# Edge stream of a graph-attention layer: node rows picked by TensorE from two float32r parts of the table, in 4 blocks by 32 sides

## The chip, the core and the metric

The kernel runs on one core of one Trainium2 chip. A core has a matrix engine (TensorE: PE for its matmuls, PEld for its weight loads), three engines for elementwise work (VectorE or DVE, ScalarE or ACT, GpSimd or POOL) and a sequencer that mostly starts transfers (SyncE or SP). They run their own instruction streams and meet at semaphores. The metric is the device time of one execution in microseconds (us). Lower is better.

## What is computed

A small language-model tower with two layers: a hashed n-gram embedding, a phase attention, a graph attention with experts, a second attention and a feed-forward part. The change lies in the graph attention. It has 16,384 nodes (16 x 1024) and 262,144 random edges, and one loop edge for each node is added:

```
h = (x_flat @ W_gat).reshape(M, HEADS, NUM_EXPERTS)        # M = 16384 nodes, 4 heads x 4
a_src = (h * att_src).sum(-1);  a_dst = (h * att_dst).sum(-1)
e = leaky_relu(a_src[src] + a_dst[dst], negative_slope=0.2)
e_max = segment_max(e, dst);  ee = exp(e - e_max[dst]);  denom = segment_sum(ee, dst)
msg = h[src] * (ee / (denom[dst] + 1e-16))[:, :, None]
agg = segment_sum(msg, dst).reshape(M, 16) + b_gat
scores = layernorm(agg).reshape(M, HEADS, NUM_EXPERTS).mean(1)   # the 2 best of 4 experts, softmax of them
out = sum over experts of g * (gelu(x @ W1[e] + b1[e]) @ W2[e] + b2[e])
```

For each of the 278,528 edges the 16 numbers of row `h[src]` are needed.

## The kernel before

**Ahead of the edge stream**, `front` makes the embedding, the first attention and the node table (24 numbers for a node: 16 of h, 4 of a_src, 4 of a_dst), and sorts the edges by their destination on VectorE. The sorted edges lie on 128 partitions, 2176 columns each. The same function holds `split(j)` (line 460), which writes 32 of the 128 table columns (tiles of 128 nodes) into `parts` for TensorE: three bf16 numbers that add up to one float32 number, made by five VectorE instructions, four times in all.

**The edge stream** (`edge_stream`, line 768) goes over the 2176 columns in 68 chunks of 32 (`CH`). A running maximum, sum and message are carried along each partition by scans. A chunk's 32 columns of rows come in two ways:

- 24 columns (`GC`) are fetched by POOL, one indirect DMA each of 128 rows of the table in DRAM (line 857). The buffer `got` holds two chunks. POOL may fill it for chunk c+2 once VectorE has let go of chunk c (`s_free`).
- 8 columns (`PC`) are picked by TensorE. A node number is written as within + 1024 x side: a place inside a block set of 8 x 128 nodes (`BLOCKS` = 8), and one of 16 sides (`SIDES`). For a column of 128 edges ScalarE makes a one-hot matrix of 1024 x 128 in bf16 (`pick`): the square of the difference between the wanted and each own number (line 871, 8 instructions for 4 columns), then relu(1 - square) (line 875, one instruction for 4 columns). TensorE multiplies it with each of the 3 parts (line 937): 8 blocks x 3 parts = 24 products of 256 columns for a column of edges, 192 for a chunk. This gives the rows of all 16 sides. VectorE multiplies them by the edge's own side (`es_own`, line 1015; `take`, line 1019), which picks one of 16, and adds over the sides (line 1021). Two columns are a `pair`, four pairs a chunk, each with a PSUM bank of its own. A pair's products wait until the take of the same pair of the chunk before has read the bank (`s_taken`).

The picked rows of chunk c+1 are made while chunk c is worked on. SyncE broadcasts the wanted numbers of a whole chunk (8 x 128 numbers to all partitions, 512 KB) into one of two halves of `away` (line 817) when ScalarE has finished with it.

**The order is written by hand**, a `turn` for each engine. On TensorE: pair 0 of the next chunk, experts 0 and 1 (`expert`, line 944, float32), pair 1, the counts of 16 columns (`count`, line 956, one-hot matrices in bf16, which VectorE makes at lines 1039 and 1040), bias and output products of the experts (lines 979 and 950), experts 2 and 3, pair 2, outputs, pair 3, the counts of 16 columns. On VectorE: scores and maximum of chunk c, one-hots for two counts, takes 0 and 1 of chunk c+1, exponentials from ScalarE, message, `s_free` (line 1077), 16 scans (line 1079), one-hots for two counts, takes 2 and 3 of chunk c+1 and their attention sums. 64 of the 68 turns carry expert work and run as a loop of two turns.

Behind the edge stream come a join of the partitions' runs and the second layer.

Of the kernel before, what the change touches and what calls it, by code (L numbers as in the profile page):

```python
# [14 lines left out]
ALU = mybir.AluOpType  # L15
ACT = mybir.ActivationFunctionType
AX = mybir.AxisListType
F32 = mybir.dt.float32
BF16 = mybir.dt.bfloat16
I32 = mybir.dt.int32  # L20
U32 = mybir.dt.uint32

P = 128
# [6 lines left out]
ST = 4  # L30
# [121 lines left out]
BLOCKS = 8  # L152
SIDES = TILES // BLOCKS
ROWS_T = CHUNKS * PC
# [19 lines left out]
def front(nc, mem, ids, tables, edges, consts, weights, sorted_keys, table_dram):  # L174
# [11 lines left out]
    hash_space, late, parts, xts = mem["hash_space"], mem["late"], mem["parts"], mem["xts"]  # L186
    with ExitStack() as ctx:
# [8 lines left out]
        low = hash_space[0:B]  # L196
# [3 lines left out]
        rows = sb("rows", [P, TILES, 3], I32)  # L200
        ring = sb("ring", [P, RINGS, 3, ST, D])
# [14 lines left out]
        rest = sb("rest", [P, BLOCKS, 4, 16])  # L216
# [179 lines left out]
        def _(dve):  # L396
# [63 lines left out]
            def split(j):  # L460

                tiles = slice(j * 32, j * 32 + 32)
                block_rows = tab[:, tiles, 0:16].rearrange("p (h k) f -> p k h f", k=BLOCKS)
                part = lambda n: parts[:, n, :, j * 64:j * 64 + 64].rearrange("p k (h f) -> p k h f", f=16)
# [130 lines left out]
            def prepare(part):  # L595

                if part == 0:
# [5 lines left out]
                    ch.step(v.tensor_scalar(few, pe_cols(key), 10, SIDES - 1, ALU.logical_shift_right, ALU.bitwise_and)); ch.settle()  # L603
# [163 lines left out]
def edge_stream(nc, mem, sorted_keys, table_dram, state_dram, y_dram):  # L767
# [6 lines left out]
    with ExitStack() as ctx:  # L774
# [8 lines left out]
        turned = pick[:, 0, 1].rearrange("p k n -> p (k n)").bitcast(F32)[:, 0:5 * P]  # L783
        own = sb("es_own", [P, PC, SIDES], F32)
        prod = sb("es_prod", [P, 2, SIDES, 16], F32)
        att = sb("es_att", [P, 2, PC, 16], F32)
# [7 lines left out]
        msg = sb("es_msg", [P, CH, 16], F32)  # L794
# [4 lines left out]
        p_got = ps("es_pgot", [P, PAIRS, 512])  # L799
# [7 lines left out]
        rows = sorted_keys[0:ROWS_T * P].rearrange("(n c) -> n c", c=PC * P)  # L807

        @block.sync
        def _(sp):  # L810
# [5 lines left out]
            def load(n, r):  # L816
# [1065 lines left out]
```

## Time and profile before

| | us |
|---|---|
| median of 3 runs | 5086.44 |
| lowest and highest | 5078.35, 5090.78 |
| the profiled execution's span | 5093.1 |
| PE busy (matmuls) | 3045.9 (60%) |
| PEld busy (weight loads) | 2318.6 (46%) |
| DVE busy | 2806.7 (55%) |
| ACT busy | 2362.3 (46%) |
| POOL busy | 2224.4 (44%) |

The profiled execution has no time of its own beside its span, which is 6.7 us above the median of the runs. A busy share says how full an engine is over the whole span. No engine is above 60%, so the shares alone don't say what sets the time. In the rows further down, "idle before, releaser" is the time in which an engine stood still ahead of an instruction, and what ended it. "issue" means that nothing in the profile released it.

### The profile page before, as it was taken

What the parts mean: (1) busy time and instruction counts of PE and PEld (TensorE: products, weight loads), DVE (VectorE), ACT (ScalarE), POOL (GpSimd) and SP (SyncE); (2) the same over time, 40 slices, a digit from 0 to 9 for tenths busy, and PEclk for the clock granted to TensorE, in tenths of its full rate; (3) what the DMA queues carried; (4) which work ended last, traced back from release to release, by engine and by line L of the source; (5) the groups of instructions that cost most, each with busy time, mean ns of one, the idle gap of its engine ahead of it and who ended that gap; (6) DMA issues with size and microseconds to landing.
All of it is one profiled execution on the core that took longest, in us unless ns stands there. A gap on an engine that the chain in (4) does not pass through costs nothing. (4 is left out here: it accounts for less than half of the span.)

```text
span 5093.1 us, 63233 instructions
## 1 busy us (share of the span) xinstructions
PE 3045.9 (60%) x21149; PEld 2318.6 (46%) x21149; DVE 2806.7 (55%) x5784; ACT 2362.3 (46%) x4288; POOL 2224.4 (44%) x2218
## 2 busy tenths in 40 slices
PE   3656663666566566566566566566566566544775
PEld 2445542554454454455455455455455455432443
DVE  8857883445445445445445445445445445467986
ACT  3636655444444444444444444444434434404886
POOL 7865613334434434434434434434434434426530
PEclk7657775777777777777777777777777777766887
DMA  1111101111111111111111111111111111112101
GB/s 58 24 22 20 22 7 44 24 23 27 31 23 27 31 23 27 31 23 27 31 23 27 31 23 27 31 23 27 31 23 27 31 23 27 25 27 75 38 19 33
DMA packets 157528, 145.13 MB, mean 28 GB/s; under 512 B 71240, under 2 KB 133080, under 8 KB 156776
## 3 DMA queue, kind: packets, MB, share of 16 engines
q1 hardware_dynamic: 88656, 109.49, 6.4%
q0 software_dynamic: 68768, 34.45, 6.2%
q8 instruction: 41, 0.67, 0.1%
q14 instruction: 63, 0.52, 0.0%
HBM read 92.97 MB, written 50.82 MB: 28 GB/s over the span
## 5 line engine op out<-in xcount | busy, mean ns | idle before, releaser
L937 PE MATMUL es_pgot<-hash_space,es_pick 128*128 128x256 bf16 x13056 | 1835.9, 288 | 1423.7 <-issue 1418.8
L857 POOL DMA_INDIRECT es_got<-node_table,late x1632 | 1548.1, 949 | 2127.0 <-DVEq L1077 1649.7
L937 PEld LDWEIGHTS es_pgot<-hash_space,es_pick 128*128 128x128 bf16 x13056 | 1302.8, 101 | 1899.6 <-issue 1742.7
L1019 DVE TENSOR_TENSOR es_prod<-es_pgot,es_own 128x512 f32<-128x512 f32 x272 | 187.7, 690 | 1801.6 <-PE es_pgot L937 1627.7
L871 ACT ACTIVATE es_pick<-es_away,consts 128x512 bf16<-128x512 f32 x1088 | 680.0, 711 | 7.0 <-DMA es_away<-sorted_keys 6.6
L293 POOL DMA_INDIRECT fr_ring<-in_emb,fr_rows x384 | 456.0, 1188 | 209.8 <-issue 112.8
L875 ACT ACTIVATE es_pick<-es_pick,consts 128x4096 bf16<-128x4096 bf16 x136 | 503.6, 3703 | 0.9
L894 ACT ACTIVATE ex_hid<-ex_phid,weights 128x256 f32<-128x256 f32 x128 | 53.6, 470 | 692.7 <-PE ex_phid L944 692.3
L1039 DVE TENSOR_TENSOR es_hot<-es_iota,late 128x1024 bf16<-128x1024 f32 x272 | 331.7, 1219 | 33.4 <-DVE es_st L1079 25.7
L1040 DVE TENSOR_TENSOR es_hot<-es_iota,late 128x1024 bf16<-128x1024 f32 x272 | 330.2, 1214 | 0.0
L894 ACT ACT_TABLE_LOAD x32 | 41.1, 1283 | 559.2 <-PE ex_phid L944 559.2
L910 ACT ACTIVATE ex_y<-ex_py 128x512 f32<-128x512 f32 x64 | 38.2, 597 | 565.0 <-remote 541.2
L1021 DVE TENSOR_REDUCE es_got<-es_prod 128x32 f32<-128x512 f32 x272 | 276.0, 1015 | 39.6
L956 PE MATMUL es_counts<-es_hot 128*128 128x128 bf16 x2176 | 202.2, 264 | 30.7 <-DVE es_hot L1040 23.8
L511 DVE TENSOR_TENSOR fr_space<-fr_space 128x1024 f32<-128x1024 f32 x173 | 211.5, 1223 | 5.4
L1079 DVE TENSOR_TENSOR_SCAN es_st<-es_ex,es_st,es_msg 128x32 f32<-128x32 f32 x1088 | 208.7, 281 | 10.0
L512 DVE TENSOR_TENSOR fr_space<-fr_space 128x1024 f32<-128x1024 f32 x173 | 210.7, 1218 | 0.0
L956 PEld LDWEIGHTS es_counts<-es_hot 128*128 128x128 bf16 x2176 | 186.0, 123 | 43.3 <-issue 33.7
L903 ACT ACT_TABLE_LOAD x64 | 82.1, 1283 | 162.0 <-PE ex_phid L944 162.0
L1347 POOL DMA_INDIRECT bk_ring<-edge_states,node_end x128 | 137.1, 1071 | 38.6 <-issue 32.4
L944 PE MATMUL ex_phid<-xc,weights 128*128 x1024 | 139.5, 279 | 0.0
L950 PE MATMUL ex_py<-weights,ex_hid 128*128 128x64 f32 x1024 | 134.9, 275 | 0.0
(351 smaller groups left out, 4294.6 us busy)
## 6 DMA issues: line engine op xcount, KB each, us to landing
es_away<-sorted_keys SPq DMA_DIRECT2D x68, 512.0 KB
es_got<-node_table,late POOLq DMA_INDIRECT x1632
edge_states<-es_st SPq DMA_DIRECT2D x68, 384.0 KB
expert_outputs<-ex_y SPq DMA_DIRECT2D x64, 256.0 KB
bk_y<-expert_outputs SPq DMA_DIRECT2D x8, 2048.0 KB
fr_ring<-in_emb,fr_rows POOLq DMA_INDIRECT x384
out_dram<-h SPq DMA_DIRECT2D x4, 1024.0 KB, 5.1
late<-in_edges SPq DMA_DIRECT2D x1, 2048.0 KB, 9.3
```

The source lines that it names most:

```text
L293: pool.indirect_dma_start(out=ring[:, r, n, t, :], out_offset=None, in_=tables[n], in_offset=bass.IndirectOffsetOnAxis(ap=rows[:, s * ST + ...
L511: ch.step(v.tensor_tensor(o[:, :, 0, :], left, right, ALU.min))
L512: ch.step(v.tensor_tensor(o[:, :, 1, :], left, right, ALU.max))
L857: pool.indirect_dma_start(out=got[:, r, k, :], out_offset=None, in_=table_dram, in_offset=bass.IndirectOffsetOnAxis(ap=src[:, n, k:k + 1]. ...
L871: a.activation(pick[:, r, half, k], away[:, r, half * 4 * P:half * 4 * P + 4 * P], ACT.Square, bias=C("away")[:, k:k + 1]).then_inc(s_act, 1)
L875: a.activation(pick[:, r, half], pick[:, r, half], ACT.Relu, scale=-1.0, bias=C("ones")).then_inc(s_pick, 1)
L937: mm = pe.matmul(p_got[:, q, c * 256:c * 256 + 256], pick[:, r, q // 2, k, at * P:at * P + P], parts[:, part, k], start=(k == 0 and part = ...
L956: mm = pe.matmul(counts, hot[:, n % 2, 0, k, :], hot[:, n % 2, 1, k, :], start=False, stop=False, skip_group_check=True)
L1021: ch.step(v.tensor_reduce(got[:, r, GC + 2 * q:GC + 2 * q + 2, 0:16], prod[:].rearrange("p c h f -> p c f h"), AX.X, ALU.add)); ch.settle()
L1039: v.tensor_tensor(hot[:, n % 2, 0], repeat(iota, OH), spread(hi[:, at], P), ALU.is_equal)
L1040: v.tensor_tensor(hot[:, n % 2, 1], repeat(iota, OH), spread(lo[:, at], P), ALU.is_equal).then_inc(s_hot, 1)
L1079: ch.step(v.tensor_tensor_scan(st[:, r, 1:, 8 + j], ex[:, 0, :, j // 4], msg[:, :, j], st[:, r, 0, 8 + j:9 + j], ALU.mult, ALU.add))
```

## The change

- The table has two parts instead of three. The first is the float32 number written as float32r (a float32 with a shortened mantissa), the second the rest, again as float32r. `split` is two VectorE instructions.
- A node number is within + 512 x side: 4 blocks of 128 and 32 sides. A product has 512 columns (32 sides x 16), which is a whole PSUM bank. A column of edges takes 4 x 2 = 8 products, a chunk 64. Both operands are float32r, the one-hot matrix too.
- The four banks of `p_got` now hold two pairs, two columns each. So pair q waits for the take of pair q-2, one chunk or half a chunk before, instead of the same pair of the chunk before.
- ScalarE makes 4 squares for 4 columns instead of 8, and the relu goes over 2048 elements for a partition instead of 4096, float32r instead of bf16.
- VectorE's take reads 2 x 512 columns instead of 2 x 256, and adds over 32 sides. The own-side mask is twice as wide.
- `away` holds one chunk in two halves, and SyncE loads halves: 256 KB each, two for a chunk.
- Places in memory: `hash_space` goes, and the hashes lie in `ring`; `msg` lies in `prod`; `turned` lies in `hot`.

The core of the diff:

```diff
-BLOCKS = 8
+BLOCKS = 4
 SIDES = TILES // BLOCKS
+SIDE_BITS = 9
+PARTS = 2
+BANKS = 4
...
-                ch.step(v.tensor_copy(part(0), block_rows)); ch.settle()
-                ch.step(v.tensor_tensor(rest[:], block_rows, part(0), ALU.subtract)); ch.settle()
-                ch.step(v.tensor_copy(part(1), rest[:])); ch.settle()
-                ch.step(v.tensor_tensor(rest[:], rest[:], part(1), ALU.subtract)); ch.settle()
-                ch.step(v.tensor_copy(part(2), rest[:])); ch.settle()
+                ch.step(v.tensor_copy(part(0), block_rows)); ch.settle()
+                ch.step(v.tensor_tensor(part(1), block_rows, part(0).bitcast(F32), ALU.subtract)); ch.settle()
...
-        away = sb("es_away", [P, 2, PC * P], F32)
+        away = sb("es_away", [P, 2, 4 * P], F32)
-        pick = sb("es_pick", [P, 2, 2, BLOCKS, 4 * P], BF16)
+        pick = sb("es_pick", [P, 2, 2, BLOCKS, 4 * P], F32R)
-        p_got = ps("es_pgot", [P, PAIRS, 512])
+        p_got = ps("es_pgot", [P, BANKS, SIDES * 16])
...
-            def load(n, r):
-                sp.dma_start(away[:, r], rows[bass.ds(n, 1), :].broadcast_to([P, PC * P])).then_inc(s_away[r], 16)
+            def load(n, half):
+                sp.dma_start(away[:, half], rows[bass.ds(n * 2 + half, 1), :].broadcast_to([P, 4 * P])).then_inc(s_away[half], 16)
...
-                    a.activation(pick[:, r, half, k], away[:, r, half * 4 * P:half * 4 * P + 4 * P], ACT.Square, bias=C("away")[:, k:k + 1]).then_inc(s_act, 1)
+                    a.activation(pick[:, r, half, k], away[:, half], ACT.Square, bias=C("away")[:, k:k + 1]).then_inc(s_act, 1)
...
-                if not first:
-                    pause(pe, s_taken, (n - 1) * PAIRS + q + 1, s_spent)
+                if not (first and q < 2):
+                    pause(pe, s_taken, n * PAIRS + q - 1, s_spent)
                 for c in range(2):
                     at = (q % 2) * 2 + c
                     for k in range(BLOCKS):
-                        for part in range(3):
-                            mm = pe.matmul(p_got[:, q, c * 256:c * 256 + 256], pick[:, r, q // 2, k, at * P:at * P + P], parts[:, part, k],
-                                           start=(k == 0 and part == 0), stop=(k == BLOCKS - 1 and part == 2))
+                        for part in range(PARTS):
+                            mm = pe.matmul(p_got[:, at], pick[:, r, q // 2, k, at * P:at * P + P], parts[:, part, k],
+                                           start=(k == 0 and part == 0), stop=(k == BLOCKS - 1 and part == PARTS - 1))
...
-                ch.step(v.tensor_tensor(prod[:], p_got[:, q].rearrange("p (c h f) -> p c h f", c=2, f=16), spread(own[:, 2 * q:2 * q + 2, :], 16), ALU.mult)); ch.settle()
+                ch.step(v.tensor_tensor(prod[:], p_got[:, q % 2 * 2:q % 2 * 2 + 2].rearrange("p c (h f) -> p c h f", f=16), spread(own[:, 2 * q:2 * q + 2, :], 16), ALU.mult)); ch.settle()
```

TensorE at the start of the edge stream, before: the products of chunk 0 in two halves, each behind its one-hot matrix (`es_pick`).

```order
L925 MATMUL es_pgot<-consts,late 128x128 x4
L925 MATMUL es_pgot<-consts,late 32x128
L937 MATMUL es_pgot<-hash_space,es_pick 128x256 [waits es_turned,es_pick]
L937 MATMUL es_pgot<-hash_space,es_pick 128x256 x95
L937 MATMUL es_pgot<-hash_space,es_pick 128x256 [waits es_pick]
L937 MATMUL es_pgot<-hash_space,es_pick 128x256 x95
L994 UNCONDITIONAL_BRANCH
```

The same place now:

```order
L932 MATMUL es_pgot<-consts,late 128x128 x4
L932 MATMUL es_pgot<-consts,late 32x128
L944 MATMUL es_pgot<-parts,es_pick 128x512 [waits es_turned,es_pick]
L944 MATMUL es_pgot<-parts,es_pick 128x512 x31
L944 MATMUL es_pgot<-parts,es_pick 128x512 [waits es_pick,es_taken]
L944 MATMUL es_pgot<-parts,es_pick 128x512 x15
L944 MATMUL es_pgot<-parts,es_pick 128x512 [waits es_taken]
L944 MATMUL es_pgot<-parts,es_pick 128x512 x15
L1001 UNCONDITIONAL_BRANCH
```

192 products of 256 columns have become 64 of 512, and the last two pairs of chunk 0 now wait for VectorE (`es_taken`).

TensorE at the start of a turn of the loop, before: pair 0 of the next chunk, experts 0 and 1 (L944), pair 1, the first count (L956).

```order
L107 ISA [waits es_pick]
L937 MATMUL es_pgot<-hash_space,es_pick 128x256 [waits es_taken]
L937 MATMUL es_pgot<-hash_space,es_pick 128x256 x47
L944 ISA
L944 MATMUL ex_phid<-xc,weights 128x128 x4
L107 REGISTER_ALU
L937 MATMUL es_pgot<-hash_space,es_pick 128x256 [waits es_taken]
L937 MATMUL es_pgot<-hash_space,es_pick 128x256 x47
L956 MATMUL es_counts<-es_hot 128x128 [waits es_hot]
```

The same place now (the names are the same, the lines 7 further down):

```order
L108 ISA [waits es_pick]
L944 MATMUL es_pgot<-parts,es_pick 128x512 [waits es_taken]
L944 MATMUL es_pgot<-parts,es_pick 128x512 x15
L951 ISA
L951 MATMUL ex_phid<-xc,weights 128x128 x4
L944 MATMUL es_pgot<-parts,es_pick 128x512 [waits es_taken]
L944 MATMUL es_pgot<-parts,es_pick 128x512 x15
L108 ISA
L963 MATMUL es_counts<-es_hot 128x128 [waits es_hot]
```

The order of the pieces is the same. A pair is 16 products instead of 48, and its wait is for another take.

SyncE in a turn of the loop, before: the wanted numbers of a whole chunk, the states, the experts' outputs.

```order
L817 ISA [waits es_pick]
L817 DMA es_away<-sorted_keys 128x1024
L107 REGISTER_ALU
L835 ISA [waits es_state]
L835 DMA edge_states<-es_st 128x768
L107 REGISTER_ALU
L838 ISA [waits es_y]
L838 DMA expert_outputs<-ex_y 128x2x256
```

SyncE now:

```order
L818 ISA [waits es_pick]
L818 DMA es_away<-sorted_keys 128x512
L108 REGISTER_ALU
L838 ISA [waits es_state]
L838 DMA edge_states<-es_st 128x768
L108 REGISTER_ALU
L818 ISA [waits es_pick]
L818 DMA es_away<-sorted_keys 128x512
L844 ISA [waits es_y]
L844 DMA expert_outputs<-ex_y 128x2x256
```

A second load, with a wait of its own, stands between the store of the states and that of the outputs.

## Rows read from the trace of the kernel before

**Rows 1.** The page's costliest groups: busy us, mean ns, idle before and releaser.

```profile
L937 PE MATMUL es_pgot<-hash_space,es_pick 128*128 128x256 bf16 x13056 | 1835.9, 288 | 1423.7 <-issue 1418.8
L857 POOL DMA_INDIRECT es_got<-node_table,late x1632 | 1548.1, 949 | 2127.0 <-DVEq L1077 1649.7
...
L1019 DVE TENSOR_TENSOR es_prod<-es_pgot,es_own 128x512 f32<-128x512 f32 x272 | 187.7, 690 | 1801.6 <-PE es_pgot L937 1627.7
```

**Rows 2.** Stretches: the loop, and one chunk of it; columns as in the first line.

```profile
core 0: us, PE busy (x) PEld busy (x) DVE busy (x) ACT busy (x) POOL busy (x), PEclk, DMA share, GB/s
930.00:4475.00 3545.00, 2186.40 (x16871) 1686.44 (x16870) 1677.66 (x3909) 1531.26 (x1752) 1480.06 (x1560) 0.75 0.12 27
...
2516.30:2571.40 55.10, 34.18 (x268) 26.68 (x266) 25.86 (x61) 25.45 (x30) 22.79 (x25) 0.75 0.13 27
```

**Rows 3.** Waits, 2000 to 3000 us: us in total, times, longest.

```profile
DVE es_prod L1019 <- PE es_pgot L937: 480.6, 24, 25.8
...
POOL es_got L857 <- DVEq L1077: 447.3, 18, 26.1
```

**Rows 4.** Timeline of that chunk: start us, us, engine, line, idle before and releaser.

```profile
2504.36 1.06 PE L944 MATMUL ex_phid<-xc,weights 128*128 x8
...
2505.26 5.40 PE L937 MATMUL es_pgot<-hash_space,es_pick 128*128 128x256 bf16 x48
...
2506.27 3.71 ACT L875 ACTIVATE es_pick<-es_pick,consts 128x4096 bf16<-128x4096 bf16 x1
...
2516.29 0.94 POOL L857 DMA_INDIRECT es_got<-node_table,late  x1 [24.45 <-DVEq L1077]
2516.86 5.00 ACT L871 ACTIVATE es_pick<-es_away,consts 128x512 bf16<-128x512 f32 x8
...
2520.51 2.02 PE L937 MATMUL es_pgot<-hash_space,es_pick 128*128 128x256 bf16 x17
...
2543.88 0.37 PE L937 MATMUL es_pgot<-hash_space,es_pick 128*128 128x256 bf16 x1 [2.44 <-issue]
...
2545.14 0.94 POOL L857 DMA_INDIRECT es_got<-node_table,late  x1 [0.30 <-issue]
...
2549.46 2.38 PE L937 MATMUL es_pgot<-hash_space,es_pick 128*128 128x256 bf16 x9 [0.33 <-issue]
...
2552.00 0.69 DVE L1019 TENSOR_TENSOR es_prod<-es_pgot,es_own 128x512 f32<-128x512 f32 x1 [25.15 <-PE es_pgot L937]
...
2571.38 0.94 POOL L857 DMA_INDIRECT es_got<-node_table,late  x1 [25.30 <-DVEq L1077]
```

**Rows 5.** Timeline, TensorE at the start of the edge stream.

```profile
846.82 6.86 PE L937 MATMUL es_pgot<-hash_space,es_pick 128*128 128x256 bf16 x44 [16.34 <-issue]
...
897.20 21.79 PE L937 MATMUL es_pgot<-hash_space,es_pick 128*128 128x256 bf16 x177 [0.31 <-issue]
```

**Rows 6.** Stretches with POOL gathering (the last one without); columns as in Rows 2.

```profile
389.20:404.20 15.00, 11.14 (x70) 9.59 (x70) 10.18 (x10) 6.74 (x16) 10.21 (x11) 0.89 0.17 28
540.80:555.80 15.00, 13.14 (x72) 11.12 (x72) 9.26 (x12) 5.53 (x19) 10.81 (x11) 0.79 0.19 31
2516.30:2531.30 15.00, 9.47 (x73) 6.93 (x70) 9.20 (x22) 6.07 (x12) 11.45 (x12) 0.85 0.17 36
2531.30:2549.50 18.20, 2.94 (x9) 0.87 (x9) 0.00 (x0) 9.97 (x11) 11.32 (x12) 0.50 0.24 52
...
2549.40:2571.30 21.90, 21.71 (x187) 18.82 (x187) 16.57 (x39) 9.31 (x9) 0.00 (x0) 0.89 0.00 0
```

**Rows 7.** Groups by shape of one chunk, VectorE: busy us, mean ns, idle before.

```profile
L1039 DVE TENSOR_TENSOR es_hot<-es_iota,late 128x1024 bf16<-128x1024 f32 x4 | 4.9, 1220 | 0.4 <-DVE es_st L1079 0.3
...
L1021 DVE TENSOR_REDUCE es_got<-es_prod 128x32 f32<-128x512 f32 x4 | 4.1, 1014 | 0.6
```

**Rows 8.** The split's scratch tile: ns of one (least, median, most), first and last start.

```profile
L467 DVE TENSOR_TENSOR fr_rest<-fr_tab,hash_space x4: 691/693/693, 350.1 to 821.6; 128x512 f32<-128x512 f32 x4
L468 DVE CAST hash_space<-fr_rest x4: 426/427/428, 350.8 to 822.3; 128x512 bf16<-128x512 f32 x4
```

More of the change, by code:

```diff
@@ L19 @@
 BF16 = mybir.dt.bfloat16
+F32R = mybir.dt.float32r
 I32 = mybir.dt.int32
@@ L185, in front @@
     c, w, h, C, W = mem["c"], mem["w"], mem["h"], mem["C"], mem["W"]
-    hash_space, late, parts, xts = mem["hash_space"], mem["late"], mem["parts"], mem["xts"]
+    late, parts, xts = mem["late"], mem["parts"], mem["xts"]
     with ExitStack() as ctx:
@@ L194, in sem @@
             return sems[-1]
-        low = hash_space[0:B]
+        rows = sb("rows", [P, TILES, 3], I32)
+        ring = sb("ring", [P, RINGS, 3, ST, D])
+        low = ring[0:B].rearrange("b r n t d -> b (r n t d)")
         triple = lambda ap: ap.rearrange("b (n t) -> b n t", n=3)
@@ L806, in edge_stream @@
         block = ctx.enter_context(nc.Block())
-        rows = sorted_keys[0:ROWS_T * P].rearrange("(n c) -> n c", c=PC * P)
+        rows = sorted_keys[0:ROWS_T * P].rearrange("(n c) -> n c", c=4 * P)
         @block.sync
@@ L824, in _, with turn @@
             load(0, 0)
-            load(1, 1)
-            sp.wait_ge(s_pick, 2)
-            load(2, 0)
-            def turn(i, with_experts, loads=2):
-                for r in range(2):
-                    if r < loads:
-                        pause(sp, s_pick, i * 4 + r * 2 + 4, s_spent)
-                        load(i * 2 + r + 3, 1 - r)
-                    pause(sp, s_state, i * 2 + r + 1, s_spent)
-                    sp.dma_start(states[:, bass.ds((i * 2 + r) * CH, CH), :], st[:, r, 1:, :]).then_inc(s_stored[r], 16)
+            load(0, 1)
+            for n in range(3):
+                sp.wait_ge(s_pick, n + 1)
+                load(1 + n // 2, n % 2)
+            def turn(i, with_experts, loads=4):
+                for r in range(2):
+                    c = i * 2 + r
+                    if r * 2 < loads:
+                        pause(sp, s_pick, c * 2 + 4, s_spent)
+                        load(c + 2, 1)
+                    pause(sp, s_state, c + 1, s_spent)
+                    sp.dma_start(states[:, bass.ds(c * CH, CH), :], st[:, r, 1:, :]).then_inc(s_stored[r], 16)
+                    if r * 2 + 1 < loads:
+                        pause(sp, s_pick, c * 2 + 5, s_spent)
+                        load(c + 3, 0)
                     if with_experts:
-                        pause(sp, s_y, i * 2 + r + 2, s_spent)
-                        sp.dma_start(y_dram.rearrange("(s t p) f -> s p t f", p=P, t=ET)[bass.ds(i * 2 + r, 1)].rearrange("s p t f -> (s p) t f"), y[:]).then_inc(s_y_out, 16)
+                        pause(sp, s_y, c + 2, s_spent)
+                        sp.dma_start(y_dram.rearrange("(s t p) f -> s p t f", p=P, t=ET)[bass.ds(c, 1)].rearrange("s p t f -> (s p) t f"), y[:]).then_inc(s_y_out, 16)
             with sp.Fori(0, ESLOTS // 2) as i:
                 turn(i, True)
-            turn(ESLOTS // 2, False, 1)
+            turn(ESLOTS // 2, False, 3)
             turn(ESLOTS // 2 + 1, False, 0)
@@ L878, in _ @@
             for n in range(2):
-                act.wait_ge(s_away[n], 16)
                 for half in range(2):
+                    act.wait_ge(s_away[half], n * 16 + 16)
                     squares(n, half)
@@ L1239, in graph_experts @@
                    node_end=sb("node_end", [P, TILES], I32))
[L1240 to L1242 removed]
+        with nc.sbuf_tensor("late", [P, 4 * COLS], I32) as late, nc.sbuf_tensor("parts", [P, PARTS, BLOCKS, SIDES * 16], F32R) as parts:
+            mem["late"], mem["parts"] = late, parts
             mem["xts"] = mem["xc"][:].rearrange("p t d -> p (t d)").rearrange("p (n t) -> p n t", t=P)
```

18 lines of the change are left out of this document (7 added, 11 removed).

## The prediction

> **What bounds the kernel now.** I read the page's groups first, then a chunk in stretches, the waits, and that chunk's timeline. The picked products (L937) are the largest group, and TensorE stands still for another 1423.7 us before them with nothing that releases it ("issue"). VectorE's take (L1019) waits 1627.7 us for them, POOL's gathers wait for VectorE [rows 1]. The loop's stretch holds 16871 matmuls [rows 2]. A chunk has 260: 192 picks, 32 counts, and 16 + 16 + 4 of the experts, whose float32 products are two matmuls each (4 products of L944 are x8 in [rows 4]). So 16871 / 260 = 65 chunks, 54.6 us each, and 3545 us of the 5093.1 lie here. In a chunk no engine is busy for more than 34.2 us [rows 2], so a wait sets it: VectorE's for TensorE (480.6 us in 1000) and POOL's for VectorE (447.3) [rows 3].
>
> The timeline shows the ring. POOL starts 24 gathers at 2516.29 and the last at 2545.14. TensorE still runs at full pace at first (17 products from 2520.51), then gives out one product in about 2.8 us ("idle 2.44 <-issue"), and is fast again from 2549.46, 4.3 us after the last gather was issued. Then comes the take of pair 3 (2552.00), VectorE works through to `s_free`, and POOL starts again at 2571.38 [rows 4]. Nothing that TensorE waits for is late in that time. It is short of instructions, and only while POOL gathers. The same is there ahead of the loop: 44 products at full pace, then next to nothing until 897.20 [rows 5]. How many it gets through: 73 in the first 15 us of a gather run, 9 in the next 18.2, and 187 in 21.9 us without gathers, 0.117 us each [rows 6]. In the stages without the edge stream, 70 and 72 float32 matmuls went through in 15 us of gathers [rows 6], so the early allowance is not special to bf16. Their late one isn't shown, as those gather runs are short.
>
> **The pieces of the change.**
>
> *TensorE, price of a product.* 48 bf16 products of 256 columns take 5.40 us less a tail, 0.11 each [rows 4]. No row has a float32r product. From below: as many columns a microsecond as bf16, 512 columns for 0.22 us. From above: like float32, where 4 products of 128 columns take 1.06 us less a tail of 0.17, 0.22 each, so 0.89 for 512. I take 0.22, the bf16 end, since the operands are numbers of a shortened mantissa, which the array needn't take apart. A chunk's picks then fall from 21.1 us (192 x 0.11) to 14.1 (64 x 0.22).
>
> The float32 row costs four times the bf16 one for as many columns. The Trainium skill, FP8 and Floating Point Precision, TensorE Precision Notes, says the same: true float32 is four passes, and there is a reduced form that reads 4-byte numbers and cuts them. It gives no time for the reduced form. One pass would leave the sum as it is, four would be the slower rival below.
>
> *TensorE, number of matmuls.* 260 become 132 (64 + 68). This is the term that decides. If the shortage goes by instructions whatever they are, a gather run of 33.2 us (2516.3 to 2549.5) still lets 73 + 9 = 82 through, and 132 - 82 = 50 remain for the time behind it. Before, 187 remained, at 0.117 each [rows 6]. Half of the 50 are picks at twice that: 25 x 0.234 + 25 x 0.117 = 8.8 us. The chunk takes 33.2 + 8.8 = 42.0 us instead of 54.6. From below, if the shortage is gone: VectorE's bound (next paragraph). From above: TensorE now often waits for one-hots or takes while instructions are to be had, and can't store many, so fewer than 82 get through. With 50 instead of 82, 82 remain, 14.4 us, 47.6 us in all.
>
> *VectorE.* Of 55.1 us it waited 25.15 for pair 3 [rows 2, 4], so its own round is 30 us. Four takes go from 512 to 1024 columns: 1.22 us (L1039 has 1024 columns) instead of 0.69, + 2.1 us [rows 1, 7]. The sum over sides is 1.014 us for 512 elements [rows 7]: doubled it adds 4.1, with the growth of the other only 2.1. I take 3.5, near the doubling. The round is 30 + 5.6 = 35.6 us, of which the small waits for TensorE may take off 1. Now VectorE is under the wait (42.0), so the 5.6 us cost nothing, and all of it if the wait goes.
>
> *ScalarE.* 8 squares are 5.00 us and the relu 3.71 [rows 4]. Half of each for 4 columns, so 17.4 us for a chunk become about 9. If float32r output costs double, nothing is won. ScalarE is busy for 25.45 of 55.1 us [rows 2], and both ways it stays below the chunk's time. Its win is worth nothing, except at the start of the stage.
>
> *POOL.* Its 24 gathers span 28.9 us from first to last, with the last one 30.1 [rows 4]. It is the floor of any chunk and stays as it is.
>
> *SyncE and the shorter bank ring.* A half of `away` is loaded again once its mask is made, a whole chunk's turn ahead, and behind it stand the stores of states and outputs. The second load waits for a relu that ScalarE makes earlier in the same turn, so it holds the outputs' store back by less than a turn's slack. Cost 0; if a load came late, ScalarE's squares would wait and pair 2 with them. Pair q now waits for take q-2. For pairs 2 and 3 that is a take in the same turn of VectorE, 10 us or more ahead of its own take: cost 0, with up to a pair's time (16 x 0.22 = 3.5 us) if this were late, which the range's upper end holds.
>
> *Ahead and behind.* A split loses one subtraction (0.69) and two casts (0.43) [rows 8], of which only the last split ends near the stage's start: 2 us. The first pair can start 4 us sooner, but of the 64 products of chunk 0 only 44 come at full pace before POOL's shortage [rows 5]; of the 177 products at 897.20 some 50 remain, twice as long: 12 us. The last two chunks: 8 us.
>
> **Sum.** 65 x (54.6 - 42.0) = 819, and 2 + 12 + 8 = 22: 841 us. 5093.1 - 841 = 4252 for the profiled execution, whose span stands 6.7 us above the runs' median: 4245 us. Its own range, from 39 to 47 us a chunk, is 4050 to 4570.
>
> **Rivals.**
>
> *The shortage is gone, VectorE sets the pace.* For: TensorE needs half as many matmuls, and late in a gather run the rows show only bf16 ones slow. Against: 132 in a chunk of 35.5 us are 3.7 a microsecond, and a gather run gave 82 / 33.2 = 2.5; POOL would gather 30 of the 35.5 us, so almost no time is left without. The time: 65 x (54.6 - 35.5) = 1242, and 60 at the ends: 5093 - 1302 - 7 = 3784, between 3680 and 3950.
>
> The Trainium skill, Runtime: NRT & Kernel Launch, Instruction fetch mechanics, has TensorE's instruction memory hold 2048 instructions, refilled ahead and mostly hidden. A loop of two chunks, some 1040 matmuls and weight loads, would fit, so by that rule there is no shortage of this kind, and its cause would be another, which the change may or may not meet. The trace shows the shortage, and that decides; but that its currency is the instruction is my reading.
>
> *Float32r streams at half the pace of bf16.* For: 4 bytes for 2. Against: nothing in the rows. The 50 products behind a gather run then take 25 x 0.47 + 25 x 0.117 = 14.7, and fewer fit in the run: 48 us. 5093 - 65 x 6.6 - 15 - 7 = 4642.
>
> *Slower: float32r is priced like float32.* 64 x 0.89 = 57 us of picks a chunk and about 8.4 for the rest (1.06 and 1.06 for 16 of its 68, [rows 4], the others alike), 66 us with TensorE never idle. 5093 + 65 x 11.4 - 7 = 5827. It decides from (54.6 - 8.4) / 64 = 0.72 us a product. For: both operands are 4 bytes. Against: a float32r number has a shorter mantissa, and I take the fourfold price to come from the longer one; no row shows it.
>
> **Chances.** The forecast 0.52, VectorE's pace 0.29, half pace 0.10, float32's price 0.05, and 0.04 for cases that I don't see, half of them without an effect. The runs lie within 0.16% of their median, so 0.3% (15 us) is about what a measurement of this kernel can tell from no change. Faster 0.93, the same 0.02, slower 0.05. The range runs from VectorE's pace to half pace, 3690 to 4640, and leaves out float32's price and the ends of the others.
>
> **What would show it.** Right: es_pgot products x4352 at about 0.22 us apart; a POOL start every 42 us; slow products with "issue" in front still there from some 15 us into a gather run until 4 to 5 us behind its last; VectorE's take waiting about 6 us a chunk for TensorE, now at pair 0 or 1. VectorE's round about 35.6 us with takes of 1.22 and about 1.9. Wrong: a POOL start every 35 or 36 us and no idle VectorE (the shortage is gone); products 0.44 or 0.89 apart; ScalarE's squares waiting for `es_away`; VectorE itself slowed by gathers, since it now issues through the whole run.

## The result, and the profile after

The changed kernel takes 4528.34 us (median of 4 runs, 4521.33 to 4549.05), the kernel before 5088.33 beside it. The ratio is 0.891, with a 95% interval from 0.889 to 0.894. So the change is faster, by 560 us, where 841 were forecast (4245 us). The profiled execution has a span of 4547.3 us. PE is busy for 2671.6 us (59%), PEld 2017.0, DVE 3204.5 (70%), ACT 1800.2 (40%), POOL 2240.7 (49%).

The page's groups after, beside [rows 1] (busy us, mean ns, idle before and its releaser; "remote" means a releaser that the profile can't name):

```profile
L863 POOL DMA_INDIRECT es_got<-node_table,late x1632 | 1561.8, 957 | 1590.0 <-DVEq L1084 1112.5
L944 PE MATMUL es_pgot<-parts,es_pick 128*128 128x512 f32 x4352 | 1369.5, 462 | 588.0 <-issue 529.4
...
L1026 DVE TENSOR_TENSOR es_prod<-es_pgot,es_own 128x1024 f32<-128x1024 f32 x272 | 332.5, 1222 | 499.6 <-remote 419.6
L1046 DVE TENSOR_TENSOR es_hot<-es_iota,late 128x1024 bf16<-128x1024 f32 x272 | 332.1, 1221 | 394.8 <-remote 315.9
...
L1028 DVE TENSOR_REDUCE es_got<-es_prod 128x32 f32<-128x1024 f32 x272 | 518.4, 1906 | 43.7 <-issue 8.6
L951 PE MATMUL ex_phid<-xc,weights 128*128 x1024 | 213.7, 323 | 462.9 <-issue 462.6
```

The picks' idle time without a releaser fell from 1418.8 us to 529.4. But the float32 products of the experts (L951) now have 462.6 of it. VectorE's idle time ahead of its takes fell from 1801.6 to 499.6, and another 394.8 us stands ahead of the one-hots (L1046).

The waits from 2000 to 3000 us, beside [rows 3] (us in total, times, longest):

```profile
POOL es_got L863 <- DVEq L1084: 346.5, 21, 23.5
...
PE ex_phid L951 <- issue: 171.5, 90, 3.1
PE es_pgot L944 <- issue: 170.1, 134, 2.4
ACT ex_hid L900 <- remote: 163.8, 7, 23.9
...
DVE es_prod L1026 <- remote: 122.8, 16, 18.6
DVE es_hot L1046 <- remote: 114.4, 19, 11.3
```

Stretches, beside [rows 2, 6]: the loop, and one chunk of it in three parts (the first 15 us of POOL's run of gathers, from there to 4.3 us behind its last gather, and the rest). The columns are the span of time, its length, each engine's busy us with its instructions, the granted clock, the DMA share, GB/s.

```profile
930.00:3950.00 3020.00, 1831.47 (x8510) 1400.08 (x8511) 2060.24 (x3900) 979.38 (x1215) 1489.90 (x1557) 0.74 0.15 31
2122.20:2137.20 15.00, 11.61 (x59) 9.15 (x58) 13.26 (x24) 6.77 (x9) 11.43 (x12) 0.89 0.36 88
2137.20:2155.40 18.20, 2.66 (x8) 1.82 (x8) 5.97 (x21) 0.00 (x0) 11.43 (x12) 0.61 0.10 9
2155.40:2168.90 13.50, 13.16 (x65) 10.41 (x65) 12.40 (x19) 6.57 (x9) 0.02 (x1) 0.77 0.00 0
```

8510 / 132 = 64.5 chunks in 3020 us, 46.8 us each. In this chunk TensorE got through 59 matmuls in the first 15 us and 8 in the next 18.2, where the kernel before had 73 and 9 [rows 6]. In the second stretch ScalarE did nothing and VectorE little. In the last one TensorE and VectorE are both nearly full.

The counts hold beyond this chunk: by their starts up to 4.3 us behind the last gather, a median of 67 matmuls got through (63 to 72 in the loop's 64 chunks), in the kernel before 76 (73 to 83).

The same chunk in the timeline (start us, us, engine, line, idle before and releaser):

```profile
2122.15 0.95 POOL L863 DMA_INDIRECT es_got<-node_table,late  x1 [16.09 <-DVEq L1084]
...
2130.25 0.61 PE L963 MATMUL es_counts<-es_hot 128*128 128x128 bf16 x8 [1.66 <-issue]
...
2131.44 5.26 PE L944 MATMUL es_pgot<-parts,es_pick 128*128 128x512 f32 x16 [0.58 <-issue]
...
2144.72 0.37 PE L951 MATMUL ex_phid<-xc,weights 128*128 x1 [2.43 <-issue]
...
2154.74 1.23 DVE L1046 TENSOR_TENSOR es_hot<-es_iota,late 128x1024 bf16<-128x1024 f32 x1 [11.27 <-remote]
...
2155.94 6.61 PE L944 MATMUL es_pgot<-parts,es_pick 128*128 128x512 f32 x16 [0.34 <-issue]
...
2156.41 0.84 ACT L900 ACTIVATE ex_hid<-ex_phid,weights 128x256 f32<-128x256 f32 x2 [23.24 <-PE ex_phid L951]
...
2168.88 0.95 POOL L863 DMA_INDIRECT es_got<-node_table,late  x1 [16.80 <-DVEq L1084]
```

The last gather of the run was issued at 2151.12. Read the rows with that in mind: TensorE is down to one product in 2.8 us, VectorE stands for 11.27 us ahead of a one-hot for which nothing is late (the counts that read its buffer ended at 2130.86), and both are back at full work 3.6 to 4.8 us behind the last gather. (ScalarE stands for 23.24 us for TensorE's `ex_phid`.) VectorE then has 12.4 us of work up to `s_free`, and only then does POOL begin again.

I call this state a shortage of instructions, since an engine stands still although what it needs is there. The name tells nothing of the cause. The instructions that the profile saw being loaded from 1000 to 2800 us, in the kernel before and in the changed one (queue, packets, MB, share):

```profile
q14 instruction: 6, 0.05, 0.0%
```

```profile
q14 instruction: 8, 0.07, 0.0%
```

That is one packet in about five chunks, and none in the chunk above. With 6 gathers instead of 24 there are 2 in the same time, so they go with POOL's gathers, which the program writes out one by one. The loops of the other engines are not loaded anew, as far as the profile records it. What holds their instructions back stays open.

### The profile page after: what moved, and what is told of

Read it like the earlier page. It is cut to its first block and busy times, and to the rows that moved or that the text cites. A ratio compares the mean times of both kernels' runs of the same rounds, so it can differ in the third digit from the quotient of the medians.

```text
span 4547.3 us, 45791 instructions
## 1 busy us (share of the span) xinstructions
PE 2671.6 (59%) x12445; PEld 2017.0 (44%) x12445; DVE 3204.5 (70%) x5772; ACT 1800.2 (40%) x3744; POOL 2240.7 (49%) x2218
## 5 line engine op out<-in xcount | busy, mean ns | idle before, releaser
L944 PE MATMUL es_pgot<-parts,es_pick 128*128 128x512 f32 x4352 | 1369.5, 462 | 588.0 <-issue 529.4
L944 PEld LDWEIGHTS es_pgot<-parts,es_pick 128*128 128x128 f32 x4352 | 965.4, 227 | 896.6 <-issue 705.1
L1026 DVE TENSOR_TENSOR es_prod<-es_pgot,es_own 128x1024 f32<-128x1024 f32 x272 | 332.5, 1222 | 499.6 <-remote 419.6
L1046 DVE TENSOR_TENSOR es_hot<-es_iota,late 128x1024 bf16<-128x1024 f32 x272 | 332.1, 1221 | 394.8 <-remote 315.9
L1028 DVE TENSOR_REDUCE es_got<-es_prod 128x32 f32<-128x1024 f32 x272 | 518.4, 1906 | 43.7 <-issue 8.6
L951 PE MATMUL ex_phid<-xc,weights 128*128 x1024 | 213.7, 323 | 462.9 <-issue 462.6
L877 ACT ACTIVATE es_pick<-es_away,consts 128x512 fp32r<-128x512 f32 x544 | 348.0, 714 | 165.6 <-DMA es_away<-sorted_keys 85.5
L951 PEld LDWEIGHTS ex_phid<-xc,weights 128*128 128x128 f32 x1024 | 179.0, 230 | 496.9 <-issue 494.2
L881 ACT ACTIVATE es_pick<-es_pick,consts 128x2048 fp32r<-128x2048 f32 x136 | 272.1, 2001 | 0.9
L1086 DVE TENSOR_TENSOR_SCAN es_st<-es_ex,es_st,es_prod 128x32 f32<-128x32 f32 x1088 | 210.1, 282 | 10.0
L957 PEld LDWEIGHTS ex_py<-weights,ex_hid 128*128 128x128 f32 x1024 | 136.4, 201 | 29.1 <-issue 23.8
```

Source lines behind the costliest of these rows:

```text
L877: a.activation(pick[:, r, half, k], away[:, half], ACT.Square, bias=C("away")[:, k:k + 1]).then_inc(s_act, 1)
L881: a.activation(pick[:, r, half], pick[:, r, half], ACT.Relu, scale=-1.0, bias=C("ones")).then_inc(s_pick, 1)
L944: mm = pe.matmul(p_got[:, at], pick[:, r, q // 2, k, at * P:at * P + P], parts[:, part, k], start=(k == 0 and part == 0), stop=(k == BLOCK ...
L951: mm = pe.matmul(p_hid[:, n % 2, t * P:t * P + P], W("e_w1_odd" if t else "e_w1")[:, n * HID:n * HID + HID], both, start=True, stop=True)
L1026: ch.step(v.tensor_tensor(prod[:], p_got[:, q % 2 * 2:q % 2 * 2 + 2].rearrange("p c (h f) -> p c h f", f=16), spread(own[:, 2 * q:2 * q + ...
L1028: ch.step(v.tensor_reduce(got[:, r, GC + 2 * q:GC + 2 * q + 2, 0:16], prod[:].rearrange("p c h f -> p c f h"), AX.X, ALU.add)); ch.settle()
```

## The experiments

A chunk's time is told below from one row of each trace: the first and the last start of VectorE's first instruction of a turn (`es_aself`, x68), 67 spacings. It is 54.1 us before (917.2 to 4540.3) and 46.3 after (892.0 to 3993.2).

The runs met different chips, and that turned out to matter. The kernel before took 5093 us beside the first group, 3398 beside the second, 5091 and 5088 beside the third and fourth, 5134 beside the fifth.

### First group: is it the gathers, and is it the count?

**Few gathers, in both kernels.** The same edit in each, with the other columns of `got` set to zero once at the start:

```diff
+FEW = 6
...
-                for k in range(GC):
+                for k in range(FEW):
                     pool.indirect_dma_start(out=got[:, r, k, :], ...)
...
+            for r in range(2):
+                ch.step(v.memset(got[:, r, FEW:GC, :], 0.0))
...
-                    pause(dve, s_landed[r], (i + 1) * (16 * GC), s_spent)
+                    pause(dve, s_landed[r], (i + 1) * (16 * FEW), s_spent)
```

> The changed kernel with 6 of a chunk's 24 gathers; the other 18 columns of got are set to zero once and stay so (their rows are left out of the computation). Everything else as it is. Theory (TensorE's and VectorE's streams are short of instructions only while POOL gathers): a gather run is 7 us long and ends before the shortage starts, so the chunk falls from 46.5 us to VectorE's round, 32 to 36 us: 4528 - 65 x 11 = 3810 us, between 3580 and 3850. Rival (the 46.5 us come of VectorE's longer round, of late half loads of away, or of the shorter bank ring, with the gathers beside it): the chunk stays at 44 us or more, 4370 to 4540 us.

> The kernel before with 6 of a chunk's 24 gathers, the other 18 columns set to zero once (their rows are left out). Theory: without the shortage TensorE's 260 matmuls take 28 us and VectorE's round 30, so the chunk falls from 54.6 us to 30 to 34 us: 5088 - 65 x 22 = 3660 us, between 3480 and 3750, below the changed kernel with as few gathers. Then the whole gain of the change comes of the shortage, and without it the change costs some 2 to 5 us a chunk. Rival (the gain comes of TensorE's shorter work, 35 us of matmuls a chunk before and 28 after, whatever POOL does): the changed kernel with few gathers stays ahead of this one by 5 us a chunk or more.

Measured: the changed kernel 3737.61 us, ratio to before 0.734 [0.732, 0.735]. The kernel before with the same edit 3460.74 us, 0.679 [0.678, 0.681]. Chunks of 34.7 and 30.6 us. The changed one, then the one before (stretches, columns as above):

```profile
1000.00:3000.00 2000.00, 1511.99 (x7574) 1230.28 (x7575) 1814.34 (x3453) 878.80 (x1090) 332.76 (x344) 0.82 0.13 36
```

```profile
1000.00:2800.00 1800.00, 1692.38 (x15257) 1482.79 (x15257) 1511.30 (x3512) 1382.95 (x1583) 338.11 (x351) 0.97 0.13 41
```

The changed kernel is bound by VectorE (1814.34 of 2000 us), the one before by TensorE (1692.38 of 1800). So without the shortage the change costs 277 us, or 4.1 us a chunk. All that it gains comes of the shortage.

**Twice as many products, the same columns.**

```diff
-                    for k in range(BLOCKS):
-                        for part in range(PARTS):
-                            mm = pe.matmul(p_got[:, at], pick[...], parts[:, part, k], ...)
+                    for w in range(2):
+                        for k in range(BLOCKS):
+                            for part in range(PARTS):
+                                mm = pe.matmul(p_got[:, at, w * 256:w * 256 + 256], pick[...], parts[:, part, k, w * 256:w * 256 + 256], ...)
```

> The changed kernel with each picked product of 512 columns made as two of 256, 128 products a chunk instead of 64, the same columns, operands and banks. Theory (the shortage counts instructions): 196 matmuls a chunk instead of 132; between 46.5 us with 132 and 54.6 with 260 that is 50.5 us: 4528 + 65 x 4 = 4790 us, between 4700 and 5050. Rival (it goes by columns or by bytes that TensorE reads): the same as the changed kernel, 4500 to 4560 us.

Measured: 5215.67 us, 1.023 [1.020, 1.026], slower than the kernel before, and above the expected 5050. A chunk takes 56.4 us. One chunk in the same three parts:

```profile
2282.90:2297.90 15.00, 8.06 (x62) 7.17 (x61) 10.51 (x22) 7.14 (x10) 11.47 (x12) 0.82 0.36 84
2297.90:2316.10 18.20, 2.91 (x12) 1.18 (x12) 0.00 (x0) 0.00 (x0) 11.34 (x12) 0.50 0.09 12
2316.10:2340.10 24.00, 20.09 (x123) 18.73 (x122) 20.96 (x39) 6.75 (x9) 0.00 (x0) 0.71 0.00 0
```

While POOL gathers, 74 matmuls get through, in the changed kernel 67, in the kernel before 82 (medians over the loop 73, 67 and 76). TensorE came off its full pace 6.5 us after the first gather, with 55 matmuls through, in the changed kernel after 14.5 us, with 59. So what runs out goes by the number of TensorE's instructions, and neither by columns nor by time.

The time is above the expected range because of VectorE, which also makes the chunk 10 us longer than the changed kernel's (the last product of pair 3, VectorE's take of pair 3, and 32 products at full pace):

```profile
2291.44 0.28 PE L945 MATMUL es_pgot<-parts,es_pick 128*128 128x256 f32 x1 [1.04 <-issue]
...
2316.94 1.23 DVE L1027 TENSOR_TENSOR es_prod<-es_pgot,es_own 128x1024 f32<-128x1024 f32 x1 [22.83 <-remote]
...
2322.79 4.07 PE L945 MATMUL es_pgot<-parts,es_pick 128*128 128x256 f32 x32
```

The take's products were there for 25 us, yet VectorE stood still. It got through 22 instructions in the run, where the changed kernel's got through 45, and so 20.96 us of work were left behind it. From 34.2 us after the first gather to POOL's next start VectorE has no idle time above 0.8 us, in any of the loop's chunks. TensorE's 123 matmuls in those 24.0 us (0.195 each, at a granted clock of 0.71; 0.117 at 0.89 before [rows 6]) run beside it. Twice TensorE waits there for VectorE's one-hots, 1.7 us each. Why more products on TensorE stop VectorE sooner stays open. The price of a product is not the reason: 32 of 256 columns take 4.07 us, 16 of 512 columns 3.88 us in the changed kernel, both at a granted clock of 1.00.

**Plain copies instead of gathers.**

```diff
-                    pool.indirect_dma_start(out=got[:, r, k, :], out_offset=None, in_=table_dram, in_offset=...)
+                    pool.dma_start(got[:, r, k, :], table_dram[k * P:k * P + P, :])
```

> The changed kernel with each of POOL's gathers of 128 picked rows replaced by a plain copy of 128 neighbouring rows of the table, also started by POOL, of the same bytes (so other rows are fetched than asked). Theory 1 (the shortage comes of POOL making the descriptors of an indirect transfer, or of the transfer's scattered reads): it goes, the chunk is 33 to 36 us, 3810 us. Theory 2 (it comes of POOL's transfers of any kind): 46 us a chunk stay if POOL's run stays near 29 us long, 4500 us.

Measured: 3743.71 us, 0.734 [0.732, 0.736], a chunk of 34.8 us, as with 6 gathers. The page:

```profile
L863 POOL DMA_DIRECT2D es_got<-node_table x1632 | 862.1, 541 | 1465.7 <-DVEq L1083 1456.3
L943 PE MATMUL es_pgot<-parts,es_pick 128*128 128x512 f32 x4352 | 1135.9, 416 | 52.0 <-DVEq L1026 39.9
```

The same bytes in as many transfers from POOL, and the shortage is gone: 52.0 us idle ahead of the picks instead of 588.0. But a copy takes POOL 541 ns instead of 957, so its run is 12 us long, not 29. In the chunk above, the first short waits of this kind stand 6 to 8 us into a run of gathers and the long ones from 15 us on, so 12 us of copies should have shown at least a little if any transfer did it. Nothing is seen. That the indirect transfers are to blame is therefore likely, but not shown: no run had copies for 29 us. Whether it would be their descriptors or their scattered reads stays open.

### Second group: a chip on which the kernel before takes 3398 us

```diff
# a_one_part
-                        for part in range(PARTS):
+                        for part in range(1):
...
-                                           start=(k == 0 and part == 0), stop=(k == BLOCKS - 1 and part == PARTS - 1))
+                                           start=(k == 0 and part == 0), stop=(k == BLOCKS - 1 and part == 0))
# a_half_sum
-                ch.step(v.tensor_reduce(got[...], prod[:].rearrange("p c h f -> p c f h"), AX.X, ALU.add))
+                ch.step(v.tensor_reduce(got[...], prod[:, :, 0:SIDES // 2].rearrange("p c h f -> p c f h"), AX.X, ALU.add))
# a_burst4, behind the gather of column k
+                    if k % 4 == 3 and k < GC - 1:
+                        pool.wait_ge(s_landed[r], 16 * (n // 2 * GC + k + 1))
```

The fourth kernel, a_no_picks, drops everything that belongs to picks and gathers the other 8 columns too.

> The changed kernel with only the first of the table's two parts multiplied (the low part of each number is left out): 32 picked products a chunk instead of 64, 100 matmuls in all. Theory (in the changed kernel's trace 66 matmuls a chunk get through the 32 us from a run's first gather, and the rest cost 0.2 us each behind it): 34 remain instead of 66, 46.5 - 32 x 0.2 = 40.1 us a chunk, 4528 - 65 x 6.4 = 4110 us, between 4000 and 4230. Rival (the distance from the forecast 42 us comes of VectorE, which is short of instructions itself, and not of TensorE's count): 44 us or more, above 4370 us.

> The changed kernel with VectorE's sum of a take over 16 of the 32 sides (the other half of the sides is left out), so four sums of about 1.0 us instead of 1.9, as many instructions. Theory (VectorE works under TensorE's wait, so its longer round costs nothing): within 1 us a chunk, 4465 to 4540 us. Rival (VectorE's longer round is on the path in part, since its waits moved): 3.6 us a chunk or most of it, 4300 to 4400 us.

> The changed kernel with POOL's 24 gathers of a chunk in six groups of 4, each group waited for until it has landed before the next is issued (some 2 to 3 us of pause each, a run of about 41 us instead of 29). Theory 1 (each pause lets TensorE's stock of instructions fill up again, and a group of 4 is over before the shortage starts): no late instructions, the chunk is then POOL's run plus its start, 41 to 45 us: 4180 to 4440 us, faster than the changed kernel. Theory 2 (the shortage starts some 6 us into any stretch with gathers and ends only when they have stopped for 4 us or more): a longer stretch short of instructions, 55 to 60 us a chunk, 5050 to 5400 us.

> The changed kernel with all 32 columns of a chunk gathered by POOL and none picked: the picked products, masks, takes and their loads are gone, the result is computed in full. TensorE keeps 68 matmuls a chunk, VectorE's round falls to some 20 us, POOL's run of gathers grows from 28.9 to about 38.8 us. Theory (the shortage counts instructions, and 66 get through a run): 2 matmuls remain behind the run, the chunk is POOL's 40 us and little more, 40 to 44 us: 4110 to 4370 us, faster than the changed kernel. Rival (a longer run is a longer shortage for whatever still has to be issued, VectorE's many small instructions too): 47 us or more, above 4550 us.

| kernel | us | ratio to before, interval | us a chunk |
|---|---|---|---|
| a_one_part | 3677.89 | 1.082 [1.081, 1.084] | 34.8 |
| a_half_sum | 3441.73 | 1.013 [1.011, 1.014] | 31.3 |
| a_burst4 | 3991.77 | 1.174 [1.172, 1.176] | 39.5 |
| a_no_picks | 4093.84 | 1.205 [1.203, 1.207] | 40.9 |

None of the expectations was made for this: there is no shortage at all, though POOL's gathers take as long (956 ns each, 24 in 29 us). ScalarE's and TensorE's waits here are for results. In a_one_part VectorE is busy for 1812.68 of 2000 us, as with few gathers, and sets the pace: it took half of the picks away and the chunk still takes 34.8. In a_half_sum, against a_one_part's chunk, VectorE's shorter sum does pay, 3.5 us, until POOL is nearly the bound (waits from 2000 to 2700 us):

```profile
POOL es_got L863 <- issue: 156.7, 514, 0.3
POOL es_got L863 <- DVEq L1084: 34.1, 22, 1.8
```

It gathers nearly without a pause there. So on such a chip VectorE's longer round, which the sum of my prediction set at nothing (and at its full price if the wait went), is on the path, and POOL's 30 us are the floor. The kernel before, at 3398 us, presumably lies near that floor; there is no trace of it on that chip. Since the shortage is absent here, a_one_part and a_half_sum do not answer what they were made for, and neither was run on a chip with the shortage.

### Third and fourth group: the same on chips with the shortage

> The changed kernel as it is, once more. In the second group of runs the kernel before took 3398 us instead of 5090, on another chip, and no stream was short of instructions there while POOL gathered. Theory (the shortage belongs to the chip that runs the program, not to the program; the gain of the change is what it saves of the shortage): where the kernel before takes about 3400 us, the changed kernel is bound by VectorE's round, 34.8 us a chunk, about 3675 us, so some 8% slower than before; where the kernel before takes about 5090 us, it takes about 4530 us again. Rival (the gain is TensorE's shorter work): faster than before on any chip.

> The changed kernel with all 32 columns of a chunk gathered and none picked, once more, since its first run (4094 us) met a chip without the shortage, where POOL's run of 40 us bounds it. Theory (the shortage counts TensorE's instructions, 66 of its 68 matmuls a chunk get through POOL's run): where the kernel before takes about 5090 us this one takes 4100 to 4370 us and is faster than the changed kernel. Rival (a longer run of gathers is a longer shortage for all engines): above 4550 us there. On a chip where the kernel before takes about 3400 us it tells nothing new: 4090 us.

Measured, on one chip: the changed kernel 4556.61 us, 0.894 [0.891, 0.897], as in the result. a_no_picks 4751.57 us, 0.932 [0.929, 0.935], slower than the changed kernel, so the expectation "2 matmuls remain" fell and the rival held. Its timeline shows why (TensorE made `ex_phid` at 1984.73):

```profile
1984.73 2.02 PE L918 MATMUL ex_phid<-xc,weights 128*128 x8
...
2014.67 0.94 POOL L844 DMA_INDIRECT es_got<-node_table,late  x1 [0.31 <-issue]
2017.34 1.28 ACT L871 ACT_TABLE_LOAD   x1 [36.81 <-remote]
...
2019.26 1.09 PE L924 MATMUL ex_py<-weights,ex_hid 128*128 128x64 f32 x4 [15.88 <-ACT ex_hid L871]
```

ScalarE's work lay ready for 30 us. It began 2.7 us after the last gather of the run was issued, and TensorE's outputs, VectorE's message and the next gathers followed it. ScalarE has few instructions a chunk and ran short all the same, so this is not TensorE's count alone: TensorE, VectorE and ScalarE are all held up, and a chain over several engines waits for whichever is held up at its place in it.

> The changed kernel with POOL's gathers in six groups of 4, each waited for until it has landed, once more. On the chip without the shortage it took 3992 us, 39.5 us a chunk, bound by POOL's pauses. Where the kernel before takes about 5090 us: theory 1 (each pause lets all engines take up instructions again, and a group of 4 is over before the shortage starts) 39 to 41 us a chunk, 3980 to 4100 us, 10% faster than the changed kernel. Theory 2 (the shortage goes on through pauses of 2 to 3 us, and ends only some 4 us behind the last gather): all of a run of 37 us is short of instructions, 50 us a chunk or more, above 4750 us, as with 32 gathers in a row.

Measured on the same chip: 4036.61 us, 0.794 [0.792, 0.795], a chunk of 39.1 us, as on the chip without the shortage (39.5). The page:

```profile
L863 POOL DMA_INDIRECT es_got<-node_table,late x1632 | 1584.6, 971 | 1073.3 <-DMA es_got<-node_table,late 637.2
L946 PE MATMUL es_pgot<-parts,es_pick 128*128 128x512 f32 x4352 | 1135.6, 417 | 51.6 <-issue 29.7
```

Theory 1 held. Five pauses a chunk of 2.0 us each (242.3 us for 120 waits from 2000 to 3000 us), and the shortage is gone: 29.7 us of "issue" ahead of the picks instead of 529.4. The same 24 gathers, spread over 38 us from the first start to the last instead of 29, give a chunk 7 us shorter. POOL starts its next run 1.25 us behind the last start of this one, so its own run with its pauses is the bound.

### Fifth group: the same two lines in the kernel before

> The kernel before with the same two lines as a_burst4: POOL's gathers in six groups of 4, each waited for until it has landed. The changed kernel went with them from 46.6 to 39.1 us a chunk (4037 us) where the kernel before takes 5090, and POOL's run with its pauses sets its pace. Theory (what the float32r picks save is the shortage alone): without it TensorE's 260 matmuls take some 29 us and VectorE's round 30, both under POOL's 39, so 39 to 40 us a chunk, 5090 - 65 x 15 = 4110 us, between 4030 and 4150, level with the changed kernel with groups. Rival (with 260 matmuls the stretches at full pace between the groups don't suffice, the count still matters): 42 us a chunk or more, above 4270 us. On a chip where the kernel before takes 3400 us: about 4000 us, and it tells only what POOL's pauses cost.

Measured: 3952.29 us, 0.771 [0.769, 0.773], a chunk of 37.6 us.

```profile
L857 POOL DMA_INDIRECT es_got<-node_table,late x1632 | 1574.0, 964 | 988.6 <-DMA es_got<-node_table,late 590.9
L939 PE MATMUL es_pgot<-hash_space,es_pick 128*128 128x256 bf16 x13056 | 1714.5, 290 | 295.9 <-issue 275.8
```

The shortage is smaller, not gone: 275.8 us of "issue" ahead of the picks instead of 1418.8. POOL's run fills the chunk all the same.

The kernel before with two more lines beats the changed kernel and also the changed kernel with the same lines (0.771 against 0.794 of the kernel before, on two chips). It is better than expected, since POOL's pauses are shorter here (231.8 us for 134 waits, 1.7 each). Of the complete kernels that were run on a chip with the shortage this is the fastest. On the other kind of chip a_burst4 was slower than the kernel before (1.174), since the pauses then buy nothing.

## Why the prediction was right, and where it was off

- **The bound** (TensorE short of instructions while POOL gathers): right on the chips with the shortage. With 6 gathers instead of 24 the kernel before needs 3461 us. That it might belong to the chip was in none of my cases, and one trace could not have shown it.
- **Instructions as the currency:** right for TensorE's share of a run. 82, 67 and 74 matmuls get through, in three kernels with quite different columns. But VectorE's share went from 22 instructions (split products) to 45 (changed kernel) with the same VectorE code, and no run explains that.
- **Product of float32r at the bf16 price:** right, 16 products in 3.88 us, 0.23 each less the tail. Not foreseen was the weight load, twice as long. The two rivals that priced float32r higher fell.
- **82 through, 50 remain, 8.8 us:** mis-sized, but not what sets the time now. 67 got through in the chunk shown and 65 remained; they took 13.5 us (0.21 each), not 8.8. One part of that is the clock: the first 16 products behind the run took 6.61 us at a granted clock of 0.56, where 16 take 3.88 at 1.00. The text had a reason for the smaller number among its bounds: TensorE waited for one-hots while it still had instructions (59 in the first 15 us instead of 73). Yet VectorE, which lets POOL go on, did not wait for these products. It stood for over 1 us ahead of 52 takes. At 51 of them (437 us together) the pair's products had ended before the wait began, and the other is the very first take. In the kernel before, the take of pair 3 stood for over 20 us in 65 chunks, and in 64 of them it started within 0.2 us of the end of its products.
- **"Now VectorE is under the wait, so the 5.6 us cost nothing": this is the step that failed.** VectorE's stream is held up too (21 instructions in 18.2 us, 11.27 us idle ahead of a one-hot), which leaves it 12.4 us of work behind the run, before `s_free`: about 33.2 + 12.4 = 45.6 us, even with all 82 matmuls through. In each of the loop's 64 chunks, in both traces of the changed kernel, VectorE has no idle time above 0.74 us from 34.2 us after the first gather until POOL starts again. A chunk takes 46.6 us on average; the 4.6 us above the forecast 42.0 are 299 us in 65 chunks, and the forecast missed by 283. I looked for what VectorE waits for and never asked whether it was short itself. Before, that was hidden by the wait for pair 3.
- **The forecast's own range** (39 to 47 us a chunk) holds the 46.6 in part by luck: its upper end was made from TensorE alone (47.6 us with 82 matmuls left).
- **The ends:** VectorE's first turn begins 25 us sooner (892.0 instead of 917.2), where 14 were set for the time ahead of the loop. Behind the last turn nothing changed (553 and 554 us).
- **VectorE's round 35.6 us:** 34.7 measured with few gathers. The take 1.22 us and the sum 1.91, as taken. The rival "VectorE sets the pace" at 3784 us is what the kernel does without the shortage (3737.61 with 6 gathers); with it, the condition of that rival (the shortage gone) was not met, though VectorE does set the pace behind a run.
- **ScalarE about 9 us of masks, POOL unchanged:** right (squares 714 ns, the relu 2001 instead of 3703; 957 ns a gather).
- **SyncE and the half loads at 0:** nearly. 85.5 of ScalarE's idle time ahead of its squares (L877) ends with a load of `es_away`, 1.3 us a chunk. What of it reaches the end was not tested alone.

What stays open: how a run of gathers holds the other engines' instructions back; what makes the difference between the chips, since the kernel, the gathers' 0.95 us each and the transfers are the same on both kinds (only one group of runs met the other kind, so that it belongs to the chip is itself not shown); and the changed kernel's own time on a chip without the shortage. VectorE's work and a_one_part's 3678 us there speak for about 3680, 8% slower than the kernel before, but that was not run.

## What to carry to other kernels

Idle time that ends with "issue" or "remote", on several engines at once and only while one of them starts indirect transfers, points to instructions held back, and not to a wait for results. To tell the two apart, look whether what the engine needed was ready before it stopped. It is cheaper to give the other streams a pause than to give them fewer instructions: five waits of 2 us a chunk did more than halving TensorE's instructions. When a cover is taken away, ask of each engine whether it was itself stopped by the same cause. And run the kernel before on more than one chip before a change is kept, since here the sign may depend on it.

## What the runs showed of the hardware

- While POOL issues 24 indirect DMAs in 29 us, the other engines are held back with their inputs ready: TensorE falls to one matmul in 2.8 us, VectorE stood 22.83 us ahead of a take and 11.27 us ahead of a one-hot, ScalarE began work that had been ready for 30 us only 2.7 us behind the last gather. In the changed kernel gathers in groups of 4 with 2 us between them don't cause it, nor do plain copies from POOL in a run of 12 us. The profile records 8 packets of instructions in 1800 us of the loop, so it is not that the loops are loaded again.
- This differed between runs on different chips: the kernel before took 5075 to 5147 us beside four groups and 3395 to 3404 beside one.
- At a granted clock of 1.00, float32r products of 512 columns follow each other in 0.23 us (16 in 3.88) and those of 256 columns in 0.12 us (32 in 4.07); bf16 products of 256 columns take 0.11 (48 in 5.40 [rows 4]). A float32r weight load takes 188 ns, a bf16 one 98 (medians). At a granted clock of 0.56, 16 float32r products took 6.61 us.
